# A second buffer for the first-layer products of a two-layer kernel, and two pieces of the attention's last product joined

## The chip, the cores and the metric

The kernel runs on one core of a Trainium2 chip. The metric is the device time of one execution in microseconds (us): 613.15 us is the median of three runs (611.65 to 616.95) before the change.

## The reference

The input is eight sequences of 512 tokens, 128 wide. Two layers follow each other. In both, the input is normalised and the result is `x + s * silu(g)`.

```python
xn = layernorm(x)
# first layer: 16 heads of 8, causal, with q and k through low-rank weights
s = softmax(mask(q @ k.T / sqrt(8))) @ v
h = gelu(xn @ w1 + b1)                      # 8 experts of 64
g = sum_e gates_e * (h_e @ w2_e + b2_e)     # the two best experts of each token
x = x + s * silu(g)
xn = layernorm(x)
# second layer: a delta rule over the tokens, one state per sequence
for t: y_t = W q_t;  W = W - 0.01 * (W k_t - v_t) k_t^T
s = norm(x) + y;  g = xn @ sign(weight).T
x = x + s * silu(g)
```

## The kernel before, in words

Work is staged by sequence. One iteration of the schedule works on several sequences at once: on `cur` it does the attention's exponentials and the products with the values, on `nxt`, one sequence ahead, the row maxima, the gates and the first-layer products, on `second`, two ahead, the first normalisation and the products q and k, on `prev` and `older` the second layer. Seven iterations use PLAN (cur is sequence 0 to 6); the head, FIRST_PLAN and LAST_PLAN stand around them.

An iteration has four groups of heads, and each group ten units. One unit is a block of scores of `nxt` for the maxima (`s_unit`, bank ps_s, line 930; VectorE takes its maxima, line 1457) and a block of scores of `cur` for the exponentials (`e_unit`, bank ps_e, lines 903 to 911; ScalarE's exponential, line 1251, writes prob). Both banks have two halves, so TensorE can be two units ahead of VectorE or ScalarE and no more.

The other work is cut into pieces, and PLAN says behind which unit (group, unit) each piece stands. Every engine runs its own share of the pieces in this one order; semaphores tie the engines together. A step (4, n) stands behind the last unit of group 3. SyncE issues all DMAs in the same order.

The pieces that the change and the prediction touch:

- pv0, pv1, pv2 (`pv`, line 939): probabilities times values of one group into bank ps_v, in three pieces, which need the exponentials of the units up to 3, 7 and 9. `yt` (line 955) turns the sums once two groups are in them; ahead of it ps_v is copied to yT, by ScalarE behind group 1 (line 1257), by VectorE behind group 3 (line 1470).
- h0 to h3 (`h`, lines 849 and 1227): one product of 512 columns each into ps_a, copied with a bias into the tile hid by ScalarE (line 1230). gelu (line 1232) then works on hid as a whole, at (4, 0).
- gb0 to gb3 (`gb`, lines 856 and 1438): the gates spread over the experts, multiplied into hid by VectorE. `out` (line 860) multiplies hid by the second weights. gt (line 841) is the gates turned.
- ps_a is one bank. Its users (A_PIECES: xnt, q, k, logits, gt, m_rows, h, v, gb, out) follow each other in the order of the schedule, and each waits until the one before it has been read.
- lev_a and lev_d, c_gram, c_u, c_y, c_r, c_kt and so on are the second layer. lev_d5 on VectorE (lines 1526 to 1531) is followed by low_blocks (line 1541, two copies), for which lev_a6 on TensorE (line 1041) waits. c_u's product is copied to u_sb by ScalarE (line 1313) for c_y (line 1109).
- k (line 820) is cast by ScalarE (line 1204) and its rest taken by VectorE (line 1401), then POOL. From the parts the stacks qst and kst of `second` are written and read back by DMA (`load_stacks`, line 439); the first unit of the next iteration waits for them.

Of the kernel before, what the change touches and what calls it, by code (L numbers as in the profile page):

```python
# [99 lines left out]
PLAN_CURRENT = ("gb0", "gb1", "gb2", "gb3", "out", "pv0", "pv1", "pv2", "yt", "x1", "m_rows1", "zero_state")  # L100
# [42 lines left out]
def iteration(second, nxt, cur, prev, older, plan=PLAN):  # L143

    for step in range(1 + max(at[0] for at in plan)):
        for u in range(UNITS):
            if step < GROUPS:
                yield "unit", (cur, nxt, step, u)
            for name in plan.get((step, u), []):
# [47 lines left out]
def two_layers(nc, x_in, W_dq, W_uq, W_dkv, W_uk, W_uv, W_o, w1_in, b1_in, w2_in, b2_in, cent_in, route_in,  # L197
# [8 lines left out]
    with ExitStack() as ctx:  # L206
# [511 lines left out]
        def _(pe):  # L718
# [383 lines left out]
            def c_y(b, c):  # L1102
# [11 lines left out]
                elif c == NT - 1 - (b.c == SEQS - 1):  # L1114
# [20 lines left out]
        def _(act):  # L1135
# [174 lines left out]
            def c_u(b, c):  # L1310
# [332 lines left out]
```

## Time and profile before

| | |
|---|---|
| median of three runs | 613.15 us (611.65 to 616.95) |
| the profiled execution | 617.68 us, its span 616.0 us |
| TensorE matmuls | 580.8 us busy (94%) |
| TensorE weight loads (overlap matmuls) | 389.4 us (63%) |
| VectorE | 391.8 us (64%) |
| ScalarE | 351.9 us (57%) |
| POOL | 171.7 us (28%) |
| mean granted TensorE clock | 0.982 |
| chain that ended last | TensorE 79%, VectorE 11%, ScalarE 4%, issue 2% |

Busy times are of the whole span. They are averages over groups that are limited by different things, so the stages of one iteration are read one by one below. PE is TensorE's matmuls, PEld its weight loads, DVE VectorE, ACT ScalarE. A matmul with float32 operands stands in the trace as two instructions.

### The profile page before, as it was taken

What the parts mean: (1) busy time and instruction counts of PE and PEld (TensorE: products, weight loads), DVE (VectorE), ACT (ScalarE), POOL (GpSimd) and SP (SyncE); (2) the same over time, 40 slices, a digit from 0 to 9 for tenths busy, and PEclk for the clock granted to TensorE, in tenths of its full rate; (3) what the DMA queues carried; (4) which work ended last, traced back from release to release, by engine and by line L of the source; (5) the groups of instructions that cost most, each with busy time, mean ns of one, the idle gap of its engine ahead of it and who ended that gap; (6) DMA issues with size and microseconds to landing.
All of it is one profiled execution on the core that took longest, in us unless ns stands there. A gap on an engine that the chain in (4) does not pass through costs nothing.

```text
span 616.0 us, 17485 instructions
## 1 busy us (share of the span) xinstructions
PE 580.8 (94%) x7289; PEld 389.4 (63%) x7289; DVE 391.8 (64%) x975; ACT 351.9 (57%) x679; POOL 171.7 (28%) x335
## 2 busy tenths in 40 slices
PE   7799989899998999899999999899998999799897
PEld 3345564567575766677666766678576777565565
DVE  4488765767667676867666685767666675412453
ACT  4412556755675476756675466656675476676231
POOL 7157022412224221432223230432224200311121
PEclk9999999999998999999998999799998999999899
DMA  4766293847252115410362014410361000000001
GB/s 113 162 153 132 44 84 90 157 63 63 74 116 48 43 29 114 97 43 10 87 118 60 10 45 98 95 44 5 83 128 41 10 12 1 26 18 2 3 3 35
DMA packets 58163, 39.42 MB, mean 64 GB/s; under 512 B 17957, under 2 KB 57988, under 8 KB 58084
## 3 DMA queue, kind: packets, MB, share of 16 engines
q1 hardware_dynamic: 58051, 38.29, 30.9%
q8 instruction: 58, 0.95, 0.7%
q14 instruction: 22, 0.17, 0.1%
q10 hardware_dynamic: 32, 0.01, 0.0%
HBM read 24.46 MB, written 9.96 MB: 56 GB/s over the span
## 4 chain that ended last, share of the span: by engine, by line
PE 79%; DVE 11%; ACT 4%; issue 2%; DMA 1%; POOL 1%; SPq 0%; DVEq 0%; POOLq 0%
PE ps_v L950 13%; PE ps_s L930 11%; PE ps_e L911 6%; PE ps_a L865 5%; PE ps_a L851 4%; PE ps_c L1015 4%; DVE cand L1457 4%; PE ps_e L903 3%; PE ps_e L907 3%; PE ps_e L738 3%; PE ps_a L820 3%; PE ps_s L933 2%; PE ps_c L1099 1%; PE ps_c L997 1%; PE ps_c L984 1%
## 5 line engine op out<-in xcount | busy, mean ns | idle before, releaser
L1457 DVE TENSOR_REDUCE cand<-ps_s 128x4 f32<-128x512 f32 (+1 forms) x320 | 213.4, 685 | 74.4 <-PE ps_s L933 45.4
L1251 ACT ACTIVATE prob<-ps_e 128x512 f32<-128x512 f32 x320 | 188.4, 598 | 97.2 <-PE ps_e L911 55.7
L930 PE MATMUL ps_s<-kst,qst 72*128 72x128 bf16 (+2 forms) x1024 | 126.4, 236 | 15.8 <-DVE cand L1457 12.0
L930 PEld LDWEIGHTS ps_s<-kst,qst 72*128 72x128 bf16 (+1 forms) x1024 | 72.1, 98 | 77.5 <-DVE cand L1457 36.5
L911 PE MATMUL ps_e<-qst,kst 75*128 75x256 bf16 (+3 forms) x416 | 105.3, 284 | 0.0
L950 PE MATMUL ps_v<-prob,vaug 128*32 128x512 f32 (+3 forms) x1024 | 90.6, 455 | 0.0
L903 PE MATMUL ps_e<-identb,negmask 128*128 128x150 bf16 (+3 forms) x320 | 73.2, 229 | 3.7 <-ACT prob L1251 3.3
L907 PE MATMUL ps_e<-qst,kst 128*128 128x128 bf16 x384 | 75.8, 223 | 0.0
L911 PEld LDWEIGHTS ps_e<-qst,kst 75*128 75x128 bf16 x416 | 40.9, 98 | 3.5
L738 PE MATMUL ps_e<-identb 128*128 128x512 bf16 x115 | 40.5, 408 | 1.9 <-POOL identb L520 1.9
L907 PEld LDWEIGHTS ps_e<-qst,kst 128*128 128x128 bf16 x384 | 38.4, 100 | 4.6 <-issue 0.3
L903 PEld LDWEIGHTS ps_e<-identb,negmask 128*128 128x128 bf16 x320 | 31.5, 99 | 14.6 <-ACT prob L1251 9.8
L950 PEld LDWEIGHTS ps_v<-prob,vaug 128*32 128x32 f32 x1024 | 24.1, 109 | 25.9 <-issue 20.3
L933 PE MATMUL ps_s<-negmask,identb 128*128 128x300 bf16 (+1 forms) x128 | 40.3, 315 | 0.0
L1015 PEld LDWEIGHTS ps_c<-second 32*32 32x32 f32 x2072 | 25.0, 107 | 21.3 <-issue 15.8
L649 POOL CAST mparts<-nm 128x32 bf16<-128x32 f32 x16 | 3.4, 211 | 121.8 <-DVE nm L1464 121.8
L865 PEld LDWEIGHTS ps_a<-w2s,hid 128*128 128x128 f32 x256 | 31.1, 192 | 7.1 <-issue 5.9
L1015 PE MATMUL ps_c<-second 32*32 32x32 f32 x2072 | 32.8, 194 | 2.5 <-DVE second L1520 1.6
L851 PE MATMUL ps_a<-xnT,w1s 128*128 128x512 f32 x64 | 33.5, 605 | 1.3 <-ACT hid L1230 0.8
L865 PE MATMUL ps_a<-w2s,hid 128*128 128x128 f32 x256 | 33.4, 283 | 0.7 <-ACT mrow L1243 0.7
L1230 ACT ACTIVATE hid<-ps_a,vecT 128x512 f32<-128x512 f32 x32 | 22.0, 687 | 17.1 <-PE ps_a L851 17.1
L687 POOL TENSOR_TENSOR second<-second,second_flat 128x512 f32<-128x512 f32 x7 | 8.9, 1266 | 60.2 <-ACT second_flat L1272 46.3
(340 smaller groups left out, 929.9 us busy)
## 6 DMA issues: line engine op xcount, KB each, us to landing
qst<-q_scratch SPq DMA_DIRECT2D x48, 192.0 KB
kst<-k_scratch SPq DMA_DIRECT2D x48, 192.0 KB
q_scratch<-qparts SPq DMA_DIRECT2D x24, 128.0 KB, 2.3
k_scratch<-kparts SPq DMA_DIRECT2D x24, 128.0 KB, 2.3
x_res<-in_L_attn_x_dram SPq DMA_DIRECT2D x8, 256.0 KB, 3.7
xn<-in_L_attn_x_dram SPq DMA_DIRECT2D x7, 256.0 KB, 3.5
out_dram<-second SPq DMA_DIRECT2D x7, 256.0 KB, 2.4
max_scratch<-mrow SPq DMA_DIRECT2D x16, 96.0 KB, 2.1
```

Of the source, the lines that this page charges most:

```text
L738: mm(ps_e[:, 1, :].rearrange("p (a c) -> p a c", c=P), identb[:, :], bcast(identb[:, :], 1, 4), start=True, stop=True, skip_group_check=True)
L851: mm(ps_a[:, :], w1s[:, 2 * c:2 * c + 2, :].rearrange("p e f -> p (e f)"), xnT[b.parity][:, :], start=True, stop=True)\
L865: mm(ps_a[:, tok(i)], hid[:, c, tok(i)], w2s[:, c, :], start=(i == 0 and c == 0), stop=False, skip_group_check=True)
L903: mm(diag, negmask[:, :], bcast(identb[:, masked:P], 1, len(todo)), start=True, stop=False, skip_group_check=True)
L907: last = mm(ps_e[:, bank, at:at + P], k[:, hd, tok(j)], q[:, hd, tok(j)], start=False, stop=True, skip_group_check=True)
L911: last = mm(ps_e[:, bank, at + own:at + TOK - P * j], k[0:SROWS, hd, tok(j)], q[0:SROWS, hd, P * j + own:TOK], start=False, stop=True, ski ...
L930: last = mm(ps_s[:, bank, w * n:w * (n + 1)], q[0:rows, hd, tok(i)], k[0:rows, hd, keys[0]:keys[1]], start=(n == 0), stop=True, skip_group ...
L933: last = mm(ps_s[:, bank, :].rearrange("p (a c) -> p a c", a=GH)[:, :, masked:P], identb[:, :], bcast(negmask[:, masked:P], 1, GH), start= ...
L950: last = mm(ps_v[32 * hh:32 * hh + 32, P * j:TOK], vaug[:, j, head_of(grp, hh), :], prob[:, u, o:o + TOK - P * j], start=(j == 0 and grp % ...
L1015: last = mm(bank[SQ * col:SQ * col + SQ, SQ * i:SQ * i + SQ], lhsT(row, col, i), rhs[SQ * row:SQ * row + SQ, i, :], start=True, stop=True, ...
L1251: af(prob[:, u, :], ps_e[:, u % 2, :], ACT.Exp).then_inc(S["e_emptied"], 1)
L1457: vec.tensor_reduce(cand[:, i, h0:h0 + FILLS * (len(hds) - 1) + 1:FILLS, S_SLOT[u]], ps_s[:, u % 2, :].rearrange("p (a c) -> p a c", a=len ...
```

## The change

The tile hid becomes two tiles, used in turn by sequence. With that, the four h pieces of `nxt` no longer have to wait until `out` of `cur` has read hid, and they move from group 3 to group 0. gb0 to gb3, out, xn2_norm, c_xn2t and gt move to later slots, v to one earlier. pv1 and pv2 are joined to one piece, pv12, which stands behind unit 2 of the next group (behind group 3: in (4, 1), after v). LAST_PLAN keeps pv1 and pv2 apart. The head and FIRST_PLAN stay as they are.

```diff
 PLAN = {
-    (0, 0): ["c_u3"], (0, 1): ["gb0"], (0, 2): ["ln2_stats", "c_y3"], (0, 4): ["ln2_rstd", "hn_norm"],
-    (0, 6): ["pv0"], (0, 7): ["c_ht", "rn", "c_out"], (0, 8): ["gb1"], (0, 9): ["pv1", "c_kt", "c_qt"],
-    (1, 0): ["load_x", "m_rows1"], (1, 1): ["c_vk", "gb2"], (1, 2): ["c_gram", "pv2"], (1, 3): ["logits"],
-    (1, 4): ["yt", "gb3", "xn2_norm", "gates"], (1, 5): ["lev_a1", "gate_norm"], (1, 6): ["pv0", "out"], (1, 7): ["lev_d1"], (1, 8): ["c_xn2t"],
-    (1, 9): ["pv1", "lev_a2", "gt"], (2, 0): ["ln1_stats", "lev_d2", "ln1_rstd", "m_parts0"], (2, 1): ["c_ffn"], (2, 2): ["ln1_norm", "lev_a3", "pv2"], (2, 3): ["lev_d3"],
+    (0, 0): ["c_u3"], (0, 1): ["h0"], (0, 2): ["ln2_stats", "c_y3", "h1"], (0, 3): ["h2"], (0, 4): ["ln2_rstd", "hn_norm", "h3"],
+    (0, 6): ["pv0"], (0, 7): ["c_ht", "rn", "c_out"], (0, 8): ["gb0"], (0, 9): ["c_kt", "c_qt"],
+    (1, 0): ["load_x", "m_rows1"], (1, 1): ["c_vk", "gb1"], (1, 2): ["c_gram", "pv12"], (1, 3): ["logits"],
+    (1, 4): ["yt", "gb2", "gates"], (1, 5): ["lev_a1", "gate_norm"], (1, 6): ["pv0", "gb3", "xn2_norm"], (1, 7): ["lev_d1"], (1, 8): ["out"],
+    (1, 9): ["lev_a2", "c_xn2t"], (2, 0): ["ln1_stats", "lev_d2", "ln1_rstd", "m_parts0"], (2, 1): ["c_ffn"], (2, 2): ["ln1_norm", "lev_a3", "pv12"], (2, 3): ["gt", "lev_d3"],
     (2, 4): ["yt", "m_rows0"], (2, 5): ["lev_a4", "xnt"], (2, 6): ["pv0", "q", "lev_d4"], (2, 7): ["turned0"], (2, 8): ["lev_a5", "k"],
-    (2, 9): ["pv1", "lev_d5", "turned1"], (3, 0): ["stacks0", "h0", "low_blocks"], (3, 1): ["lev_a6"], (3, 2): ["h1", "lev_d6", "pv2"], (3, 3): ["c_u0"],
-    (3, 4): ["h2", "yt", "c_y0"], (3, 5): ["c_r1"], (3, 6): ["pv0", "c_u1"], (3, 7): ["c_y1", "h3"], (3, 8): ["c_r2"],
-    (3, 9): ["c_u2", "pv1"], (4, 0): ["m_parts1", "gelu", "stacks1"], (4, 1): ["pv2", "c_y2"], (4, 2): ["v"], (4, 3): ["yt", "x1", "c_r3"],
+    (2, 9): ["lev_d5", "turned1"], (3, 0): ["stacks0", "low_blocks"], (3, 1): ["lev_a6"], (3, 2): ["lev_d6", "pv12"], (3, 3): ["c_u0"],
+    (3, 4): ["yt", "c_y0"], (3, 5): ["c_r1"], (3, 6): ["pv0", "c_u1"], (3, 7): ["c_y1"], (3, 8): ["c_r2"],
+    (3, 9): ["c_u2"], (4, 0): ["m_parts1", "gelu", "stacks1"], (4, 1): ["v", "pv12", "c_y2"], (4, 3): ["yt", "x1", "c_r3"],
 }
...
-        hid = sb("hid", [P, NC, TOK])
+        hid = [sb(f"hid{p}", [P, NC, TOK]) for p in range(2)]
...
-            def pv(b, grp, piece):
-                if piece == 0:
+            def pv(b, grp, pieces):
+                if 0 in pieces:
...
-                pe.wait_ge(S["e_emptied"], b.count(GROUPS * UNITS, UNITS * grp + (4, 8, 10)[piece]))
-                for j, u0, at in (((0, 0, 0),), ((1, 4, 0), (3, 4, 384)), ((2, 8, 0),))[piece]:
+                pe.wait_ge(S["e_emptied"], b.count(GROUPS * UNITS, UNITS * grp + (4, 8, 10)[pieces[-1]]))
+                for j, u0, at in [tile for n in pieces for tile in (((0, 0, 0),), ((1, 4, 0), (3, 4, 384)), ((2, 8, 0),))[n]]:
...
-                last.then_inc(S["pv_used"], 1)
+                last.then_inc(S["pv_used"], len(pieces))
```

In `h`, `gelu`, `gb` and `out_piece`, `hid` becomes `hid[b.parity]`.

## Rows read from the trace of the kernel before

**Rows 1.** The page, busy time, share of the span and instructions of each engine.

```profile
PE 580.8 (94%) x7289; PEld 389.4 (63%) x7289; DVE 391.8 (64%) x975; ACT 351.9 (57%) x679; POOL 171.7 (28%) x335
```

**Rows 2.** Busy time by stage: stretch, its length, busy us, PEclk, DMA share, GB/s.

```profile
114.60:127.40 12.80, 11.25 (x99) 6.52 (x97) 9.62 (x24) 8.65 (x15) 6.01 (x8) 1.00 0.63 112
251.00:264.30 13.30, 11.51 (x114) 7.22 (x112) 10.51 (x27) 8.64 (x16) 6.54 (x9) 1.00 0.36 84
299.70:318.40 18.70, 18.70 (x181) 13.27 (x180) 11.18 (x24) 12.93 (x22) 1.88 (x5) 1.00 0.49 104
318.40:333.30 14.90, 13.12 (x115) 7.62 (x113) 10.67 (x27) 8.74 (x16) 6.57 (x9) 0.89 0.41 75
387.40:403.80 16.40, 14.61 (x115) 8.90 (x113) 10.74 (x27) 9.03 (x16) 6.61 (x9) 0.79 0.33 67
```

**Rows 3.** Timeline, group 0 of cur 4: start us, duration us, instruction, [idle before <-releaser].

```profile
320.63 0.10 PEld L903 LDWEIGHTS ps_e<-identb,negmask 128*128 128x128 bf16 x1 [0.30 <-ACT prob L1251]
...
322.78 0.66 DVE L1593 TENSOR_TENSOR second<-ps_c,second 128x512 f32<-128x512 f32 x1
...
324.09 0.39 PE L930 MATMUL ps_s<-kst,qst 72*128 72x256 bf16 x2 [1.67 <-DVE cand L1457]
```

**Rows 4.** Timeline, group 3: a last piece alone, then both pieces, each with what follows.

```profile
304.26 0.64 PE L950 MATMUL ps_v<-prob,vaug 128*32 128x256 f32 x8
...
304.83 0.40 PE L930 MATMUL ps_s<-kst,qst 128*128 128x128 bf16 x4
...
314.33 1.50 PE L950 MATMUL ps_v<-prob,vaug 128*32 128x384 f32 x24
...
315.76 0.49 PE L1109 MATMUL ps_c<-u_sb,vk 128*128 128x128 f32 x2
```

**Rows 5.** Timeline from k's product (2,8) to lev_a6 (3,1), TensorE and VectorE.

```profile
296.19 1.12 PE L820 MATMUL ps_a<-xnT,w_k 128*128 128x512 f32 x2
...
297.15 0.39 PE L930 MATMUL ps_s<-kst,qst 72*128 72x128 bf16 x4
...
297.77 1.07 PE L950 MATMUL ps_v<-prob,vaug 128*32 128x384 f32 x16
...
298.06 0.69 DVE L1401 TENSOR_TENSOR krest<-ps_a,kparts 128x512 f32<-128x512 f32 x1 [0.78 <-ACT kparts L1204]
...
298.67 0.68 DVE L1457 TENSOR_REDUCE cand<-ps_s 128x4 f32<-128x512 f32 x1
298.77 0.59 PE L1015 MATMUL ps_c<-second 32*32 32x32 f32 x24
...
299.92 1.02 PE L851 MATMUL ps_a<-xnT,w1s 128*128 128x512 f32 x2
...
300.77 0.39 PE L930 MATMUL ps_s<-kst,qst 128*128 128x128 bf16 x4
...
300.94 0.45 DVE L1541 COPY second<-second 32x128 f32<-32x128 f32 x2
...
301.49 0.66 PE L1041 MATMUL ps_c<-second 64*64 64x64 f32 x8
```

**Rows 6.** Timeline, h3 and ScalarE's copy of it.

```profile
311.55 1.02 PE L851 MATMUL ps_a<-xnT,w1s 128*128 128x512 f32 x2
...
312.62 0.69 ACT L1230 ACTIVATE hid<-ps_a,vecT 128x512 f32<-128x512 f32 x1 [0.82 <-PE ps_a L851]
```

**Rows 7.** Timeline behind group 3: VectorE's copy of ps_v, and v.

```profile
315.90 0.69 DVE L1470 COPY yT<-ps_v 128x512 f32<-128x512 f32 x1 [1.06 <-PE ps_v L950]
...
316.31 1.06 PE L829 MATMUL ps_a<-w_v,xnT 128*128 128x128 f32 x8
```

**Rows 8.** Timeline, step (3,4): the copy of c_u0's product, and h2.

```profile
306.14 0.26 ACT L1313 COPY u_sb<-ps_c 128x128 f32<-128x128 f32 x1
...
306.19 1.07 PE L851 MATMUL ps_a<-xnT,w1s 128*128 128x512 f32 x2
```

**Rows 9.** Timeline, TensorE, first unit of the iteration with cur 1.

```profile
114.27 0.38 PE L930 MATMUL ps_s<-kst,qst 128*128 128x128 bf16 x4 [1.01 <-issue]
```

More of the change, by code:

```diff
@@ L99 @@
 PLAN_OLDER = ("c_u3", "c_y3", "c_out")
-PLAN_CURRENT = ("gb0", "gb1", "gb2", "gb3", "out", "pv0", "pv1", "pv2", "yt", "x1", "m_rows1", "zero_state")
+PLAN_CURRENT = ("gb0", "gb1", "gb2", "gb3", "out", "pv0", "pv1", "pv2", "pv12", "yt", "x1", "m_rows1", "zero_state")
 SEQUENCES = 8
@@ L159, in iteration @@
                 if of is not None:
-                    yield name, (of, step) if name in ("pv0", "pv1") else (of, step - 1) if name in ("pv2", "yt") else (of,)
+                    yield name, (of, step) if name in ("pv0", "pv1") else (of, step - 1) if name in ("pv2", "pv12", "yt") else (of,)
 def schedule():
@@ L864, in out_piece @@
                     for c in range(NC):
-                        mm(ps_a[:, tok(i)], hid[:, c, tok(i)], w2s[:, c, :], start=(i == 0 and c == 0), stop=False,
+                        mm(ps_a[:, tok(i)], hid[b.parity][:, c, tok(i)], w2s[:, c, :], start=(i == 0 and c == 0), stop=False,
                            skip_group_check=True)
@@ L1117, in _ @@
             pieces = {"xnt": xnt, "q": lambda b: qk(b, 0), "k": lambda b: qk(b, 1), "v": v, "logits": logits, "gt": gt,
-                      "out": out_piece, "m_rows0": lambda b: m_rows(b, 0), "m_rows1": lambda b: m_rows(b, 1), "pv0": lambda b, grp: pv(b, grp, 0), "pv1": lambda b, grp: pv(b, grp, 1), "pv2": lambda b, grp: pv(b, grp, 2), "yt": yt, "c_xn2t": c_xn2t, "c_ht": c_ht, "c_kt": c_kt,
+                      "out": out_piece, "m_rows0": lambda b: m_rows(b, 0), "m_rows1": lambda b: m_rows(b, 1), "pv0": lambda b, grp: pv(b, grp, (0,)), "pv1": lambda b, grp: pv(b, grp, (1,)), "pv2": lambda b, grp: pv(b, grp, (2,)), "pv12": lambda b, grp: pv(b, grp, (1, 2)), "yt": yt, "c_xn2t": c_xn2t, "c_ht": c_ht, "c_kt": c_kt,
                       "c_qt": c_qt, "c_vk": c_vk, "c_gram": c_gram, "c_ffn": c_ffn}
@@ L1229, in h @@
                 after(act, S["gelu_ready"], b.count(1, 0))
-                af(hid[:, c, :], ps_a[:, :], ACT.Identity, bias=vecT[:, c:c + 1]).then_inc(S["a_emptied"], 1)
+                af(hid[b.parity][:, c, :], ps_a[:, :], ACT.Identity, bias=vecT[:, c:c + 1]).then_inc(S["a_emptied"], 1)
             def gelu(b):
                 act.wait_ge(S["a_emptied"], A_NUMBER[b.c, "h3"] + 1)
-                af(hid[:, :, :], hid[:, :, :], ACT.Gelu).then_inc(S["gelu_ready"], 1)
+                af(hid[b.parity][:, :, :], hid[b.parity][:, :, :], ACT.Gelu).then_inc(S["gelu_ready"], 1)
             def out_piece(b):
@@ L1315, in _ @@
             pieces = {"xnt": xnt, "q": lambda b: split_hi(b, 0), "k": lambda b: split_hi(b, 1), "v": v, "gates": gates, "gt": gt,
-                      "gelu": gelu, "out": out_piece, "m_rows0": lambda b: m_rows(b, 0), "m_rows1": lambda b: m_rows(b, 1), "pv2": pv, "c_xn2t": c_xn2t, "c_ht": c_ht, "c_kt": c_kt,
+                      "gelu": gelu, "out": out_piece, "m_rows0": lambda b: m_rows(b, 0), "m_rows1": lambda b: m_rows(b, 1), "pv2": pv, "pv12": pv, "c_xn2t": c_xn2t, "c_ht": c_ht, "c_kt": c_kt,
                       "c_qt": c_qt, "c_gram": c_gram, "c_ffn": c_ffn}
@@ L1440, in gb @@
                 dve.wait_ge(S["gelu_ready"], b.count(1, 1))
-                vec.tensor_tensor(hid[:, c, :], hid[:, c, :], ps_a[:, :], ALU.mult).then_inc(S["a_emptied"], 1)
+                vec.tensor_tensor(hid[b.parity][:, c, :], hid[b.parity][:, c, :], ps_a[:, :], ALU.mult).then_inc(S["a_emptied"], 1)
             def out_piece(b):
```

2 lines of the change are left out of this document (1 added, 1 removed).

## The prediction

> **What bounds the kernel now.** I read the busy shares first: TensorE is busy for 94% of the span, so time is won only where it stands idle, where its clock is low, or where its work shrinks [rows 1]. Then the stages of one iteration of the plan (busy time by stage): group 3 is full to the last tenth (18.70 of 18.70 us), group 0 is not (11.51 of 13.30). The granted clock is 1.00 in all of them but four group 0 stretches: 0.89 in three, 0.79 in one [rows 2]. A stretch at 0.89 takes 14.90 us against 13.30, the one at 0.79 takes 16.40: together 3 x 1.6 + 3.1 = 7.9 us lost to the clock.
>
> The timeline of group 0 shows the hole. Behind the third unit VectorE does the statistics of the residual, then c_y3's addition (0.66 us), and only then the maxima for which the sixth unit waits: TensorE stands idle for 1.67 us. The same gap is there in five iterations (cur 2 to 6), and in four of them the clock then fell. A smaller gap, 0.30 us, stands ahead of unit 2's mask product: ScalarE is late after gelu and its table loads [rows 3].
>
> **The change, term by term.** Matmuls are moved, not saved: four h products, one gt, one gb leave one group for another. Only waits, the clock and the joins count.
>
> *Joins.* A middle piece alone takes 1.00 us from its start to the next product (297.77 to 298.77), a last piece 0.57 (304.26 to 304.83), both in a row 1.43 (314.33 to 315.76) [rows 4, 5]. Group 3 has them in a row already. So 3 groups x 7 iterations save 0.14 each: **-2.9 us** (bounds 0 and, by busy time, 1.07 + 0.64 - 1.50 = 0.21 each, -4.4).
>
> *Group 0 gets the h's.* They fill both gaps: -1.97 us. But hid has two buffers and ps_a still one bank. From an h product's start to its copy by ScalarE is 1.07 us, the copy 0.69, a release about 0.05: h can follow h after 1.8 us [rows 6], while the work between, one h (0.85) and one unit (0.6), is 1.45 [rows 5]. So h2 and h3 wait 0.35 each, h1, with c_y3 ahead of it, 0.15: +0.85. And v now stands ahead of pv12. Before, v covered VectorE's copy of yT (0.69, begun 0.14 after c_y2's start) ahead of the transposes yt; now only c_y2's two products do (0.55): +0.35 [rows 4, 7]. Net -0.8, times 5; cur 1 has other gaps, I take -0.4: **-4.4** (bounds -8, if nothing new waits, and 0).
>
> *Group 3 loses the h's, and pv1 goes from (2,9) to (3,2).* This decides. lev_a6 in (3,1) needs low_blocks, VectorE's two copies, and already starts 0.10 us after them (301.39 to 301.49), in every iteration with a k behind it (cur 1 to 5). Back from there is a chain which the change doesn't touch: k's product 296.19, ScalarE's cast, VectorE's rest (298.06), the maxima of unit (2,9) (298.67), lev_d5's three, the maxima of (3,0), the copies. It takes 5.30 us. TensorE's work in that stretch was just that long; without pv1 (1.00) and h0 (0.85) it is 0.96 + 0.62 + 1.15 + 0.72 = 3.45 [rows 5]. So 1.85 us is not saved but waited, about 0.5 ahead of unit (3,1)'s first product (it needs the maxima of (2,9)), the rest ahead of lev_a6: 5 x 1.85 = 9.2. cur 6 has no k: between 0 and 1.85, I take 1.0, since the rest and the cast drop out. h1 and h3 come out at full value. Behind h2 stands c_y0, which needs the copy of u that ends 306.40, while TensorE would be there at 306.19: +0.25, times 6, 1.5 [rows 8]. Together **+11.7** (bounds 2, if VectorE ran ahead, and 14).
>
> *The first iteration (cur 0).* Its group 3 ends in a wait of 1.01 us for a release that the view does not name; the code's wait there is for the stacks of sequence 2 [rows 9]. Their start hangs on k, not on group 3. What leaves group 3 (four h 3.4, pv1 1.0, less the join's 0.9 and the yt wait) is then waited: +3.2, and the three waits among h's in group 0 add 0.8: **+4.0** (bounds 0, if gaps in groups 1 and 2 take it up, and 5).
>
> *At nothing.* gb, xn2_norm, out, c_xn2t one or two slots later: VectorE catches up under out's products; without that cover, at most 0.35 an iteration, 2 us in all. gt in (2,3) has m_rows0 a unit behind. On SP the load of x_res goes with gb0 past the store of c_out and its wait for POOL: load_x and the row maxima's write then stand behind one more issue, and all three are used a group or more later. POOL's order is unchanged. ScalarE's wait for pieces at unit 4 stands behind the joined piece in TensorE's order, so it adds none.
>
> The Trainium skill (TensorE: Matmul & The Clock Gate, section "A second HAM failure mode: psum-queue depth-cycling") says that brief idles between groups of matmuls, come by in cycling through PSUM banks, can be frequent enough to make the clock swing. By that rule the h's, turning about one bank, would keep group 0's low clock; by the rows, where short gaps left it at 1.00, they would not.
>
> **Rivals.**
> 1. *The clock holds in group 3*: the split stalls are too short. +8.4 - 7.9 + 1.6 = +2.1, 615.3 to 619.8: 617. For it: no contiguous gap there reaches 1.67. Against: some 1.85 us idle within 2.6. Chance 0.24.
> 2. *The stall at lev_a6 does not come, and it is faster.* VectorE would have to reach low_blocks some 1.8 us sooner, which it can only if k's cast and rest come sooner against TensorE. Its place is 298.06 to 301.39. Then the third term is 1.5, or some 2: -2.9 - 4.4 + 2 + 4.0 - 7.9 + 1.6 = -7.6, 605.6 to 610: 607. It decides from a stall under 0.5. Against: five of five iterations show copies and lev_a6 0.10 to 0.15 apart. That h's in group 3 took ScalarE from that chain is not so: h0's copy comes after it. Chance 0.16.
> 3. *The clock falls after every lev_a6 stall*: 2.5 x 1.6 more: 625. Chance 0.15.
> 4. *The clock falls in group 0 all the same*, by a run of short gaps between h's: six times 1.6 on the forecast, 631. (This is what the page's rule would do.) Against: gap by gap there is 0.4 or less. Chance 0.05.
> That the change doesn't do what it says: in group 3 the join joins nothing, and it is counted so.
>
> **The numbers.** Forecast 621, chance 0.40; by itself 617 to 626. About 1% (607.0 to 619.3) is what a measurement here can't tell from no change. Within it lie rival 1 (0.24), the low end of the forecast (0.05) and what of rival 2 ends above 607 (0.06): 0.35. Slower: 0.35 + 0.15 + 0.05 = 0.55. Faster: 0.10. The range 611 to 629 leaves out most of rival 2 and rival 4.
>
> **What would show it.** In the profile after: lev_a6 still 0.1 us behind low_blocks, with idle TensorE before it, some 1.8 us in group 3 of cur 1 to 5; group 0 with h products 1.8 us apart, no 1.67 us gap, clock 1.00; the third and second piece 24 in a row in all groups, 1.43 us; a wait of about 4 us ahead of cur 1's first unit; yt waiting about 0.35 us for yT. Wrong, if group 3 has TensorE busy throughout, or if the clock in it stays at 1.00 after each stall.

## The result, and the profile after

The changed kernel is slower, by 1.5 to 1.8%. In the first set its four runs gave 632.89 us in the median (622.68 to 637.33) beside 615.05 for the kernel before (611.65 to 617.18); two of the four, the profiled one among them, lie more than 1.5% above the fastest and are left out of the ratio, 1.0178 (95% interval 1.0115 to 1.0241). A second set gave 622.66 (621.30 to 628.74) beside 615.06, ratio 1.0147 (1.0092 to 1.0201). The forecast was 621 with a range of 611 to 629: the side and the second set are in it, and so is the mean of the first set's two other runs, 625.9; the first set's median is not. So there are two things to explain: why it is slower at all, and why the same kernel takes 622 us in one execution and 637 in another.

The profiled execution took 636.67 us (span 634.9, before 616.0). The page of the changed kernel, first the engines' busy time (it answers to [rows 1]), then the granted clock in 40 slices:

```profile
PE 591.2 (93%) x7289; PEld 399.4 (63%) x7289; DVE 394.4 (62%) x975; ACT 350.1 (55%) x679; POOL 170.7 (27%) x335
...
PEclk9899999899979998999979998999979999999999
```

The stages of the changed kernel (stretch, length, busy us of the engines, PEclk, DMA share, GB/s), in order: group 0 of cur 1, group 0 and group 3 of cur 3, group 0 and group 3 of cur 4. They answer to [rows 2]:

```profile
118.40:133.90 15.50, 15.13 (x91) 8.32 (x89) 9.40 (x23) 9.81 (x17) 4.83 (x7) 0.89 0.55 93
267.30:281.80 14.50, 14.02 (x107) 8.33 (x105) 10.33 (x26) 10.83 (x19) 6.50 (x9) 1.00 0.32 55
316.80:338.40 21.60, 19.79 (x189) 14.17 (x188) 12.13 (x27) 11.21 (x21) 2.67 (x6) 0.84 0.48 103
338.40:352.90 14.50, 14.02 (x107) 8.31 (x104) 10.34 (x26) 10.83 (x19) 6.50 (x9) 1.00 0.25 53
387.90:408.20 20.30, 18.30 (x190) 13.13 (x188) 12.12 (x27) 11.19 (x21) 2.67 (x6) 0.92 0.49 110
```

The picture of [rows 2] is turned round. Group 0, four h pieces longer, now runs at 1.00 in cur 2 to 6. Group 3, which was full before (18.70 of 18.70), has 1.8 to 2.0 us without TensorE and runs at 0.84 or 0.92 in all five iterations cur 1 to 5. Its length in cur 3 is 21.6 us although four h pieces have left it.

The timeline of the changed kernel (start, duration, instruction, idle before it and what ended it) shows, in order: the wait that opens cur 1, a hole in the middle of lev_a2's products in cur 1, three of the h pieces in group 0 of cur 3, then the chain from k to lev_a6 and the transposes yt at the end of that group 3.

```profile
115.16 0.66 PE L960 MATMUL ps_v<-ident,yT 128*128 128x128 f32 x4 [0.81 <-DVE yT L1470]
118.09 0.38 PE L930 MATMUL ps_s<-kst,qst 128*128 128x128 bf16 x4 [2.28 <-issue]
...
151.89 0.45 PE L1015 MATMUL ps_c<-second 32*32 32x32 f32 x30
155.31 0.24 PE L1015 MATMUL ps_c<-second 32*32 32x32 f32 x2 [2.97 <-issue]
...
268.72 1.02 PE L851 MATMUL ps_a<-xnT,w1s 128*128 128x512 f32 x2
...
270.52 1.13 PE L851 MATMUL ps_a<-xnT,w1s 128*128 128x512 f32 x2
...
272.42 1.13 PE L851 MATMUL ps_a<-xnT,w1s 128*128 128x512 f32 x2 [0.17 <-ACT hid L1230]
...
314.29 1.12 PE L820 MATMUL ps_a<-xnT,w_k 128*128 128x512 f32 x2
...
316.17 0.69 DVE L1401 TENSOR_TENSOR krest<-ps_a,kparts 128x512 f32<-128x512 f32 x1 [0.78 <-ACT kparts L1204]
...
316.78 0.68 DVE L1457 TENSOR_REDUCE cand<-ps_s 128x4 f32<-128x512 f32 x1
...
316.40 0.40 PE L930 MATMUL ps_s<-kst,qst 128*128 128x128 bf16 x4
...
317.52 0.40 PE L930 MATMUL ps_s<-kst,qst 128*128 128x128 bf16 x4 [0.34 <-DVE cand L1457]
...
319.04 0.45 DVE L1541 COPY second<-second 32x128 f32<-32x128 f32 x2
...
319.60 0.65 PE L1041 MATMUL ps_c<-second 64*64 64x64 f32 x8 [1.30 <-issue]
320.18 0.58 PE L930 MATMUL ps_s<-kst,qst 128*128 128x128 bf16 x4
...
322.48 2.79 PE L950 MATMUL ps_v<-prob,vaug 128*32 128x384 f32 x24
...
336.25 0.49 PE L1109 MATMUL ps_c<-u_sb,vk 128*128 128x128 f32 x2
...
337.13 0.66 PE L960 MATMUL ps_v<-ident,yT 128*128 128x128 f32 x4 [0.17 <-DVE yT L1470]
```

From k's product to lev_a6 it is 319.60 - 314.29 = 5.31 us, against 5.30 in [rows 5]: the chain on VectorE is what it was, and TensorE, with pv1 and h0 gone from between, waits for it twice, with 0.34 and 1.30 us of idle time. These figures count from the end of the product before, which the profile models; counted from start to start, less the work between as [rows 5] has it (0.62 for a unit, 0.72 for the one ahead of lev_a6), the waits are 317.52 - 316.40 - 0.62 = 0.50 and 319.60 - 317.52 - 0.72 = 1.36 us. Right behind the second wait the products run at half speed: four score products take 0.58 us where [rows 4] has 0.40, and the joined pieces 2.79 where it has 1.50.

### The profile page after: what moved, and what is told of

It is laid out like the page before. It is cut to its first block, busy times and chain, and to the rows that moved or that the text cites. A ratio compares the mean times of both kernels' runs of the same rounds, so it can differ in the third digit from the quotient of the medians.

```text
span 634.9 us, 17485 instructions
## 1 busy us (share of the span) xinstructions
PE 591.2 (93%) x7289; PEld 399.4 (63%) x7289; DVE 394.4 (62%) x975; ACT 350.1 (55%) x679; POOL 170.7 (27%) x335
## 4 chain that ended last, share of the span: by engine, by line
PE 77%; DVE 7%; ACT 7%; issue 4%; DMA 2%; POOL 1%; SPq 0%; ACTq 0%; DVEq 0%
PE ps_v L950 13%; PE ps_s L930 11%; PE ps_e L911 6%; PE ps_a L865 5%; PE ps_a L851 5%; PE ps_c L1015 3%; PE ps_s L933 3%; PE ps_e L903 3%; PE ps_e L907 3%; PE ps_e L738 2%; ACT hid L1230 2%; ACT prob L1251 2%; PE ps_a L820 2%; PE ps_c L997 1%; PE ps_c L1099 1%
## 5 line engine op out<-in xcount | busy, mean ns | idle before, releaser
L930 PEld LDWEIGHTS ps_s<-kst,qst 72*128 72x128 bf16 (+1 forms) x1024 | 75.3, 100 | 74.9 <-DVE cand L1457 31.2
L950 PE MATMUL ps_v<-prob,vaug 128*32 128x512 f32 (+3 forms) x1024 | 89.0, 468 | 0.0
L907 PE MATMUL ps_e<-qst,kst 128*128 128x128 bf16 x384 | 74.3, 220 | 0.0
L950 PEld LDWEIGHTS ps_v<-prob,vaug 128*32 128x32 f32 x1024 | 26.9, 115 | 24.9 <-issue 21.1
L933 PE MATMUL ps_s<-negmask,identb 128*128 128x300 bf16 (+1 forms) x128 | 42.5, 332 | 0.0
L851 PE MATMUL ps_a<-xnT,w1s 128*128 128x512 f32 x64 | 36.2, 647 | 4.2 <-ACT hid L1230 3.5
L1230 ACT ACTIVATE hid<-ps_a,vecT 128x512 f32<-128x512 f32 x32 | 22.0, 687 | 22.0 <-PE ps_a L851 21.7
```

The source lines that it names most:

```text
L851: mm(ps_a[:, :], w1s[:, 2 * c:2 * c + 2, :].rearrange("p e f -> p (e f)"), xnT[b.parity][:, :], start=True, stop=True)\
L907: last = mm(ps_e[:, bank, at:at + P], k[:, hd, tok(j)], q[:, hd, tok(j)], start=False, stop=True, skip_group_check=True)
L930: last = mm(ps_s[:, bank, w * n:w * (n + 1)], q[0:rows, hd, tok(i)], k[0:rows, hd, keys[0]:keys[1]], start=(n == 0), stop=True, skip_group ...
L933: last = mm(ps_s[:, bank, :].rearrange("p (a c) -> p a c", a=GH)[:, :, masked:P], identb[:, :], bcast(negmask[:, masked:P], 1, GH), start= ...
L950: last = mm(ps_v[32 * hh:32 * hh + 32, P * j:TOK], vaug[:, j, head_of(grp, hh), :], prob[:, u, o:o + TOK - P * j], start=(j == 0 and grp % ...
```

## The experiments

Entries of the plan that stay as they are, are left out of the diffs.

**Undoing one half of the change each.** The theory: the stall ahead of lev_a6 is the sum of the two pieces taken from between, h0 and pv1. The first kernel is the changed one with the four h pieces back in group 3.

```diff
-    (0, 1): ["h0"], (0, 2): ["ln2_stats", "c_y3", "h1"], (0, 3): ["h2"], (0, 4): ["ln2_rstd", "hn_norm", "h3"],
+    (0, 2): ["ln2_stats", "c_y3"], (0, 4): ["ln2_rstd", "hn_norm"],
...
-    (3, 0): ["stacks0", "low_blocks"], (3, 2): ["lev_d6", "pv12"], (3, 4): ["yt", "c_y0"], (3, 7): ["c_y1"],
+    (3, 0): ["stacks0", "h0", "low_blocks"], (3, 2): ["h1", "lev_d6", "pv12"], (3, 4): ["h2", "yt", "c_y0"], (3, 7): ["c_y1", "h3"],
```

> The changed plan with the four h pieces back in their old slots of group 3, the joined piece and all else as changed. Theory A (the loss is idle time ahead of lev_a6, which VectorE's chain from k sets, and the low clock behind it): h0's 0.85 us covers that stall again, pv1's 1.0 does not; so 0.9 to 1.0 us idle ahead of lev_a6 in cur 1 to 5, the 1.67 us hole of group 0 back, no wait of over 1.1 us at the start of cur 1. About 3 us slower than before to 3 us faster (joins -2.9, stall +5, less low clock in group 3 than in the changed kernel). Theory B (the loss is the h's turning about one bank in group 0): as before or faster by the joins, 612 or less, and the stall ahead of lev_a6 plays no part.

Measured: 621.61 us (614.78 to 626.92), ratio 1.0076 (1.0031 to 1.012). The second kernel keeps the h pieces in group 0 and takes the join apart again.

```diff
-    (0, 9): ["c_kt", "c_qt"], (1, 2): ["c_gram", "pv12"], (1, 9): ["lev_a2", "c_xn2t"], (2, 2): ["ln1_norm", "lev_a3", "pv12"],
-    (2, 9): ["lev_d5", "turned1"], (3, 2): ["lev_d6", "pv12"], (3, 9): ["c_u2"], (4, 1): ["v", "pv12", "c_y2"],
+    (0, 9): ["pv1", "c_kt", "c_qt"], (1, 2): ["c_gram", "pv2"], (1, 9): ["pv1", "lev_a2", "c_xn2t"], (2, 2): ["ln1_norm", "lev_a3", "pv2"],
+    (2, 9): ["pv1", "lev_d5", "turned1"], (3, 2): ["lev_d6", "pv2"], (3, 9): ["c_u2", "pv1"], (4, 1): ["v", "pv2", "c_y2"],
```

> The changed plan with pv1 and pv2 apart again in their old slots, the h pieces in group 0 as changed. Theory A: pv1 in (2,9) covers 1.0 us of the 1.85, so about 0.85 us idle is left ahead of lev_a6, too short for the clock to fall there; group 0 stays filled at a clock of 1.00; the wait at the start of cur 1 stays over 2 us. About 612 to 617, well below the changed kernel. Theory B (the bank in group 0): no better than the changed kernel's fast runs, 622 and more. Theory C (joining as such costs, by a longer stretch of TensorE without a unit): faster than the changed kernel, with the stall ahead of lev_a6 as long as there.

Measured: 620.38 us (618.26 to 620.78), ratio 1.0048 (1.001 to 1.0087). The timeline of the kernel with the h pieces back, the sixth unit of group 0, then the unit ahead of lev_a6 and lev_a6 of the same iteration:

```profile
256.44 0.39 PE L930 MATMUL ps_s<-kst,qst 72*128 72x256 bf16 x2 [1.88 <-DVE cand L1457]
...
299.12 0.39 PE L930 MATMUL ps_s<-kst,qst 128*128 128x128 bf16 x4
...
300.83 0.65 PE L1041 MATMUL ps_c<-second 64*64 64x64 f32 x8 [0.95 <-issue]
```

And of the kernel with the pieces apart, two h pieces in group 0, then the unit ahead of lev_a6 and lev_a6:

```profile
264.25 1.13 PE L851 MATMUL ps_a<-xnT,w1s 128*128 128x512 f32 x2 [0.17 <-ACT hid L1230]
...
266.16 1.12 PE L851 MATMUL ps_a<-xnT,w1s 128*128 128x512 f32 x2 [0.26 <-ACT hid L1230]
...
310.25 0.39 PE L930 MATMUL ps_s<-kst,qst 128*128 128x128 bf16 x4
...
311.83 0.65 PE L1041 MATMUL ps_c<-second 64*64 64x64 f32 x8 [0.81 <-issue]
```

Counted from start to start as above, lev_a6 waits 0.99 us without pv1 (idle 0.95), 0.86 without h0 (idle 0.81), and 0.50 + 1.36 = 1.86 without both: the parts add up, and the prediction had 1.00 + 0.85. That shows where the stall comes from. In neither kernel did the clock fall in group 3. Each half of the change is slower by itself, in the median by less than the whole. Both times are misses: I expected 612 to 618 and 612 to 617. In the profile of the second kernel an undisturbed iteration takes 68.1 us against 67.4 to 67.5 before, and cur 0 and cur 1 are 4.4 and 2.9 us longer than before; the largest differences lie in those two. The second time lies between what theories A and B gave and does not decide between them; the rows do, with the stall as theory A had it.

**Taking the stall away from VectorE's side.** The changed kernel with the two copies low_blocks issued ahead of k's rest.

```diff
-    (2, 7): ["turned0"], (3, 0): ["stacks0", "low_blocks"],
+    (2, 7): ["low_blocks", "turned0"], (3, 0): ["stacks0"],
```

> The changed kernel with VectorE's two copies low_blocks moved from (3,0) to (2,7), where VectorE is idle; they need lev_d4 alone. Nothing else is touched, and TensorE's order is the same. Theory A: lev_a6 then waits only for lev_d5's first operation, so the gap ahead of it goes from 1.27 us to 0.2 or less in cur 1 to 5, the clock holds in group 3, and the kernel is at 606 to 612, faster than both. Theory B (the bank in group 0) and theory C (the join): 622 or more, since neither is touched.

Measured: 622.14 us (616.88 to 624.34), ratio 1.0111 (1.0076 to 1.0146): a miss. Its timeline in group 3 of one iteration:

```profile
306.61 0.40 PE L930 MATMUL ps_s<-kst,qst 128*128 128x128 bf16 x4 [0.23 <-DVE cand L1457]
...
307.93 0.40 PE L930 MATMUL ps_s<-kst,qst 128*128 128x128 bf16 x4 [0.54 <-DVE cand L1457]
...
308.64 0.68 PE L1041 MATMUL ps_c<-second 64*64 64x64 f32 x8
...
309.60 0.40 PE L930 MATMUL ps_s<-kst,qst 128*128 128x128 bf16 x4 [0.28 <-DVE cand L1457]
```

lev_a6 no longer waits, but the maxima behind k's rest are still as late, and the units wait for them: 0.23 + 0.54 + 0.28 us. low_blocks was the last link, not the cause: wherever the wait stands, TensorE has too little work beside VectorE's chain there. The clock stays at 1.00 in group 3 in this profile, and an iteration with cur 2 to 5 takes 67.8 us.

**Holding the clock in the stall.** The changed kernel with seven bfloat16 products of 512 columns into ps_a behind unit (3,0), read by nobody.

```diff
-    (3, 0): ["stacks0", "low_blocks"],
+    (3, 0): ["stacks0", "spare", "low_blocks"],
...
+            def spare(b):
+                pe.wait_ge(S["a_emptied"], A_NUMBER[b.c, "k"] + 1)
+                for _ in range(7):
+                    mm(ps_a[:, :].rearrange("p (a c) -> p a c", c=P), identb[:, :], bcast(identb[:, :], 1, 4), start=True, stop=True,
+                       skip_group_check=True)
```

> The changed kernel with seven products of 512 columns (bfloat16, into the free bank ps_a, read by nobody) behind unit (3,0) for cur 0 to 5. No wait goes and no work is saved; they only keep TensorE busy in the stall ahead of lev_a6. Theory A with the clock: the stall's idle time shrinks to 0.3 or less, the clock stays at 1.00 in group 3, lev_a6 starts as late after k as in the changed kernel: 615 to 619, below the changed kernel although it does more. If the low clock in group 3 has another cause, it stays, and the time is that of the changed kernel, 623 to 637.

Measured: 624.63 us (623.96 to 626.66), ratio 1.0145 (1.0104 to 1.0185). Two stretches of it, group 3 of cur 3 and the whole iteration with cur 3:

```profile
314.30:333.10 18.80, 18.14 (x197) 13.18 (x196) 12.18 (x27) 11.24 (x21) 2.67 (x6) 1.00 0.53 118
...
264.80:333.10 68.30, 67.08 (x916) 48.30 (x914) 48.40 (x121) 42.78 (x83) 19.21 (x34) 1.00 0.28 64
```

The clock stays at 1.00 in group 3 of cur 2 to 5, and the four runs spread over 2.7 us where those of the changed kernel spread over 14.7 and 7.4 in its two sets. That fits a spread that goes with the clock in group 3, but does not show it: the kernel with low_blocks early held that clock in its profile too, and its six runs spread over 7.5. And the median is above the 615 to 619 that I expected, and no lower than that of the second set of the changed kernel: a miss. With the clock held, an iteration takes 68.3 us against 67.4 before. This kernel, too, had a hole in lev_a2 of cur 1, 3.45 us long, with the lower clock behind it: its cur 0 and cur 1 take 59.3 and 76.5 us, against 55.5 and 67.4 in the profile of the kernel before. These 12.9 us are more than the 8.9 by which its whole span is longer. So the clock in group 3 is not all that makes the change slow.

**The changed kernel again**, unaltered.

> The changed kernel once more, unaltered, to see how often its clock falls behind the stall at lev_a6. My theory: the stall of 1.25 us and the smaller one of 0.3 us ahead of it are there in cur 2 to 5 of every execution; what differs between executions is for how long the clock is at 0.5 behind them, so the time goes down as the mean granted clock goes up, 622 us at 0.995 and 636 us at 0.967. Rival (the time differs for another reason, such as the wait that opens cur 1): an execution whose profile has a clock above 0.985 still takes over 630 us.

Measured: 622.66 us; the profiled execution 622.25, span 620.5. Group 3 of cur 2, 3 and 4 in it, then the whole iteration with cur 5:

```profile
237.00:258.70 21.70, 19.89 (x190) 14.10 (x189) 12.18 (x27) 11.25 (x21) 2.68 (x6) 0.84 0.48 102
308.10:328.50 20.40, 18.40 (x191) 13.21 (x189) 12.24 (x27) 11.30 (x21) 2.68 (x6) 0.92 0.52 110
377.90:396.70 18.80, 16.80 (x191) 12.41 (x188) 12.18 (x27) 11.24 (x21) 2.68 (x6) 1.00 0.53 118
396.70:465.00 68.30, 65.74 (x909) 47.54 (x907) 48.43 (x121) 42.79 (x83) 19.26 (x34) 1.00 0.27 64
```

In all three stretches of group 3 TensorE idles 1.8 to 2.0 us (in cur 4, with the clock at 1.00, it is 0.34 and 1.30 ahead of lev_a6, as in cur 3 of the first profile), and yet the clock fell for long, for short and not at all: 21.7, 20.4 and 18.8 us. That gives the price of a fall from rows, 1.6 or 2.9 us. The hole in lev_a2 is not there in this execution. My expectation that time goes by the clock alone holds only in part: 621.30 us stands beside a clock of 0.994 and 622.25 beside 0.982.

**The clock's share in the kernel before.** The kernel before with the same seven products (they wait for gb0 here) in the hole of group 0.

```diff
-    (0, 4): ["ln2_rstd", "hn_norm"],
+    (0, 4): ["spare", "ln2_rstd", "hn_norm"],
```

> The kernel before, with seven bfloat16 products of 512 columns into ps_a behind unit (0,4), read by nobody, where TensorE stood idle for 1.67 us. It has no change of the plan. My theory (the change's only large gain in group 0 was the clock): the gap is at most 0.4 us, the clock is 1.00 in group 0 of cur 2 to 6, group 0 takes 13.3 us in every iteration, the time is 606 to 610 us (five stretches of 1.6 us less at most). Rival: the clock falls elsewhere instead, or the fall cost nothing that lasts: 612 to 616 us.

Measured: 612.06 us (610.21 to 612.35), ratio 0.9941 (0.9921 to 0.9961), above the 606 to 610 that I expected and in the range of the rival. Group 0 of cur 1 and of cur 5, and the iteration with cur 3:

```profile
116.30:130.30 14.00, 12.60 (x106) 7.18 (x104) 10.40 (x26) 9.71 (x17) 6.39 (x8) 1.00 0.49 110
...
387.40:400.80 13.40, 13.13 (x122) 7.92 (x120) 10.59 (x27) 8.75 (x17) 6.57 (x9) 1.00 0.38 80
...
252.50:320.00 67.50, 67.10 (x917) 47.74 (x914) 47.87 (x121) 43.03 (x83) 19.35 (x34) 1.00 0.28 64
```

An iteration is as long as an undisturbed one before, the clock is at 1.00 in all of cur 1 to 6, and group 0 of cur 2 to 6 takes 13.4 us, where the profiled execution before had 14.8, 13.4, 14.9, 16.4 and 14.9: its four falls cost 7.5 us, close to the 7.9 that the prediction read there. The time fell by less for two reasons that are not the clock's in these groups. The products also stand in cur 1, where the gaps are smaller, and group 0 of cur 1 takes 14.0 us against 12.8 in [rows 2]. And cur 0 began 1.5 us later in this execution than in the other, so that the profiled span is only 5.6 us shorter. In the median, filling the hole was worth 3.0 us net of its cost in cur 1, some 4.3 without it (an estimate from the two rows).

**Moving only as much as the hole holds.** The changed kernel with two h pieces in group 0 and two in group 3, and with pv1 and pv2 of group 2 apart in their old places.

```diff
-    (0, 1): ["h0"], (0, 2): ["ln2_stats", "c_y3", "h1"], (0, 3): ["h2"], (0, 4): ["ln2_rstd", "hn_norm", "h3"],
+    (0, 2): ["ln2_stats", "c_y3", "h0"], (0, 3): ["h1"], (0, 4): ["ln2_rstd", "hn_norm"],
...
-    (2, 9): ["lev_d5", "turned1"], (3, 0): ["stacks0", "low_blocks"], (3, 2): ["lev_d6", "pv12"], (3, 4): ["yt", "c_y0"], (4, 1): ["v", "pv12", "c_y2"],
+    (2, 9): ["pv1", "lev_d5", "turned1"], (3, 0): ["stacks0", "h2", "low_blocks"], (3, 2): ["lev_d6", "pv2"], (3, 4): ["h3", "yt", "c_y0"], (4, 1): ["pv12", "c_y2"], (4, 2): ["v"],
```

> The changed kernel, but only two of the four h pieces go to group 0 (h0 behind unit (0,2) and h1 behind (0,3), where the gap ahead of the sixth unit was); h2 stands in group 3 where h0 was (3,0), h3 where h2 was (3,4). pv1 of group 2 is back at (2,9) and pv2 at (3,2); the other two groups keep the joined piece. My theory (the changed kernel is slow because TensorE has nothing to do while VectorE goes from k's rest to low_blocks, and because its clock falls in that gap): lev_a6 waits 0.1 us or less in cur 1 to 5, the gap of 1.67 us in group 0 is filled, the clock stays at 1.00 in both groups, an iteration without a fallen clock takes 65.5 to 66.5 us against 67.4 before, the time is 600 to 608 us. Rival A (the gain is eaten by the turn about the bank ps_a and by VectorE's later start in group 1): the stall at lev_a6 goes and the clock holds, but an iteration takes 67 us or more, the time is 610 to 614 us. Rival B (the stall of some 3 us inside lev_a2 of cur 1 and the wait that opens cur 1 are what costs): the time stays above 616 us.

Measured: 606.05 us (602.62 to 606.49), ratio 0.9845 (0.9811 to 0.988): 1.5% faster than the kernel before, and faster than the changed one. The copies and lev_a6 in its timeline, and the iteration with cur 3:

```profile
302.32 1.02 PE L851 MATMUL ps_a<-xnT,w1s 128*128 128x512 f32 x2
...
303.35 0.45 DVE L1541 COPY second<-second 32x128 f32<-32x128 f32 x2
...
303.90 0.66 PE L1041 MATMUL ps_c<-second 64*64 64x64 f32 x8
```

```profile
253.90:319.60 65.70, 64.98 (x908) 47.32 (x906) 48.20 (x121) 42.73 (x83) 19.35 (x34) 1.00 0.29 67
```

lev_a6 follows the copies by 0.1 us after their end and waits for nothing; the iteration is 1.7 us shorter than an undisturbed one before, and TensorE is idle for 0.7 us of it. The iterations cur 2 to 6 all stand at 1.00. Three things differ from the changed kernel at once (two h pieces, pv1 of group 2, the place of v), so the run does not say what each is worth; both rivals fell with it.

The same kernel with group 2's pieces joined at (3,2) and low_blocks at (2,7):

```diff
-    (2, 7): ["turned0"], (2, 9): ["pv1", "lev_d5", "turned1"], (3, 0): ["stacks0", "h2", "low_blocks"], (3, 2): ["lev_d6", "pv2"],
+    (2, 7): ["low_blocks", "turned0"], (2, 9): ["lev_d5", "turned1"], (3, 0): ["stacks0", "h2"], (3, 2): ["lev_d6", "pv12"],
```

> As the kernel with two h pieces in group 0, but group 2's middle and last piece are joined at (3,2) as in the changed kernel, and VectorE's two copies low_blocks go from behind (3,0) to behind (2,7), ahead of k's rest in VectorE's order. My theory: lev_a6 no longer hangs on the chain from k, so the joined piece costs no stall, and the join gives 0.14 us an iteration: 599 to 608 us, the same as the kernel with two h pieces or 1 us below it. Rival A: TensorE then waits for the maxima of unit (2,9) ahead of unit (3,1), which hang on the same rest of k: a gap of 0.5 us there and 0.3 us in group 2, and 3 to 5 us more than the kernel with two h pieces.

Measured: 604.47 us (602.25 to 605.39), ratio 0.9826 (0.9796 to 0.9857), not to be told from the one above. Its iteration takes 66.1 us, 0.4 more and not 0.14 less: of the rival's waits the one in group 2 came (0.3 us there). What its profiled execution gains, 2.7 us, lies ahead of cur 0, which began 3.9 us earlier, and in cur 1 (0.7 us), not in the join.

**The hole in lev_a2 of cur 1.** The trace puts no releaser to it ("issue"). In the stretch around it (148 to 156 us of the first profile) the DMA queues of the changed kernel hold:

```profile
q1 hardware_dynamic: 2487, 0.63, 92.3%
q8 instruction: 1, 0.02, 1.3%
```

Up to the hole the DMA engines are full with the load of the constant rows of the second pair of stacks (qst from identb, kst from negmask, 1.7 MB), in the hole they are busy for 0.49 of the time, and one packet of instructions, 16 KB, is among the others. Four kernels move that load to an earlier place:

```diff
-                if half and b.c < 2:
-                    load_pads(b.parity)
+                if b.c == 0:
+                    load_pads(1 - half)
```

> The changed kernel; only the load of the constant rows of the second pair of stacks (qst from identb, kst from negmask, 1.7 MB) is issued one iteration and a half sooner, behind m_rows0 of the first sequence, so that it no longer falls into group 1 of cur 1. My theory (the stall of some 3 us inside lev_a2 of cur 1 comes because TensorE's next instructions are fetched by the same DMA engines that this load keeps full): no gap over 0.5 us in groups 1 and 2 of cur 1, and those two groups take 35.5 us, as in the execution of the changed kernel that had no such gap, against 40.1 in the one that had; the rest, with the stall at lev_a6, stays; 619 to 626 us, by the clock. Rival (the gap has to do with the order of the work in cur 1, not with this load): a gap of 1.5 to 3.5 us stays in lev_a2 or lev_a3 of cur 1, and the time is that of the changed kernel.

> The kernel with two h pieces in group 0, with the same earlier load of the constant rows. My theory: the gap of 2.66 us in group 1 of cur 1 and the low clock behind it go, 4 us in all; the iterations with cur 2 to 5 stay at 65.7 us: 600 to 604 us. Rival (the load only moves the trouble): the first iteration gets longer by as much, since the load then falls beside the loads of the head, and the time stays at 605 to 607 us.

> The kernel with two h pieces in group 0 and the copies low_blocks ahead of k's rest, with the same earlier load. Its iterations take 66.1 us against 65.7 of the kernel with the copies in their old place, its gap in cur 1 was 1.64 us. My theory: 600 to 604 us, and with equal starts 1.5 to 2 us slower than the kernel with the copies in their old place. Rival (the old place of the copies costs something at the end of the first iteration, where it was 1.5 us slower): it stays 1 to 2 us faster.

> A control: the kernel before, with the earlier load alone. Its trace had no gap in cur 1 behind that load. My theory: cur 1 stays as it was, no change within 0.4%: 613 to 616 us. Rival (the load also slows what comes after it in the kernel before, such as the wait of 0.9 us in group 0 of cur 1 or the one ahead of cur 1): 609 to 612 us.

Measured, each above what I expected: the changed kernel with it 629.15 us (626.46 to 630.83), ratio 1.0207 (1.0165 to 1.025); the one with two h pieces 604.11 (598.38 to 605.53), 0.9787 (0.9737 to 0.9837); with the early copies 605.27 (601.72 to 609.64), 0.9827 (0.9775 to 0.9878); the kernel before 619.43 (612.88 to 624.91), 1.0052 (1.0016 to 1.0087). Group 1 of cur 1 in the first of them:

```profile
130.90:150.20 19.30, 19.30 (x272) 15.37 (x270) 13.73 (x36) 9.55 (x22) 3.42 (x8) 1.00 0.03 7
```

TensorE is busy throughout, and no hole is there in any of the three profiles with h pieces in group 0; without the move it was there in five of seven (1.64 to 3.45 us; with two h pieces it stands in c_xn2t, right behind lev_a2). The hole was absent twice without the move, and no record says that TensorE waited for that packet. But the traces hold more. These are the rows from the start of the span to just ahead of the hole's end, for the changed kernel and for the one with the seven products in group 3:

```profile
0.00:155.20 155.20, 137.44 (x1104) 80.24 (x1104) 97.55 (x229) 73.32 (x135) 52.23 (x130) 0.98 0.62 105
...
0.00:157.40 157.40, 139.45 (x1104) 80.69 (x1104) 97.63 (x229) 73.31 (x135) 52.10 (x130) 0.98 0.61 104
```

In both, and with low_blocks early, TensorE has run 1104 matmuls and 1104 weight loads when it stops, in the two kernels with two h pieces 1103 and 1104, although different work stands there: the 31st of lev_a2's 32 matmuls, the 24th where seven were put in ahead, the second of c_xn2t where two h pieces fewer stand ahead. So the hole has its place in the count of TensorE's instructions, not in the order of the work, which was the rival. And in each of the five a packet of instructions lands 1.2 to 1.4 us before the hole ends; it starts 17.6 to 20.8 us after the packet before it on its queue, against 11.7 to 16.1 us in the nine profiles without a hole. That the next instructions came late is thus well supported. That the load made them late agrees with the three profiles that moved it, but why they were in time twice without the move stays open. The changed kernel did not get faster: its clock fell behind all five stalls this time (groups 1 and 2 of cur 1 take 35.4 us, as expected). And the trouble moved, as the rival had it. With two h pieces the wait that opens cur 1 is now

```profile
118.17 0.59 PE L930 MATMUL ps_s<-kst,qst 128*128 128x128 bf16 x4 [5.58 <-issue]
```

against some 1 us without the move. The intervals of the four kernels with two h pieces overlap, so none of them is shown to be the best. Why the kernel before got 0.5% slower is open.

## Why the prediction was right, and where it was wrong

**The side and the main step held.** Left aside the clock, an iteration of cur 2 to 5 was to get -0.42 (joins) - 0.8 (group 0) + 1.85 + 0.25 (group 3) = +0.88 us longer. It is 68.3 us against 67.4 in two undisturbed iterations, +0.8 from the starts to two places (68.26 and 67.47):

```profile
251.00:318.40 67.40, 65.48 (x908) 47.03 (x906) 47.76 (x121) 42.93 (x83) 19.36 (x34) 1.00 0.28 65
```

is that row of the kernel before, beside the last row of the changed kernel's second profile above. Lengths of groups and iterations are from the start of a first unit to that of the next. By groups 0 to 3 the two iterations differ by +1.07, -0.38, +0.06 and +0.04 us: group 3 is as long as before without its four h pieces. Step by step, with the waits counted from start to start as the prediction counted them:

- *Joins*, 0.14 us each: groups 1 and 2 take 0.13 less in the changed kernel than with the pieces apart (19.08 against 19.21, 15.93 against 16.06).
- *Group 0*: h follows h after 1.80 and 1.90 us (1.8 predicted). The second h, with c_y3 ahead of it, waits for nothing where 0.15 stood; the third and fourth come 0.45 us later than the 1.45 of work between them, where 0.35 stood. The transposes yt start 337.13 - 336.25 = 0.88 us behind c_y2, whose products take 0.55: they wait 0.33 us for yT, 0.35 predicted. The gap of 1.67 us is gone and the clock is 1.00 in cur 2 to 6, so rival 4 fell. The Trainium skill (TensorE: Matmul & The Clock Gate, section "A second HAM failure mode: psum-queue depth-cycling") describes brief idles, from cycling through PSUM banks, that are frequent enough to make the clock swing. Applied to the h's turn about the one bank ps_a, it would have had the clock come down; these rows, with 0.48 us idle in 14.5 us and a clock of 1.00, speak against it here.
- *Group 3*: 1.86 us of stall against 1.85 (rival 2 fell), split 0.50 and 1.36 where 0.5 and 1.35 stood; c_y0 waits 0.36 against 0.25. In cur 6, which has no k, TensorE idles 0.66 us ahead of lev_a6 and 0.54 ahead of lev_d5's products, 1.2 together where 1.0 stood.
- *The first iteration*: the waits at its end are 0.81 + 2.28 us against some 4; from the start of cur 0 to that of cur 1 it takes 57.8 us (57.6 in the second profile) against 55.5. +2.3 measured, +3.6 with the join predicted. Behind that wait the clock fell for 3.4 us, as the +1.6 of the sum had it.

**The term that was mis-sized is the clock in group 3.** The step "I take half of five, 2.5 x 1.6 = +4.0" failed in both factors. The clock fell behind 13 of the 15 stalls of three profiles (five, three, five), and it often stayed low for twice as long: with the prices from above, 1.6 + 4 x 2.9 = 13 us in the first profile and about 6 in the second (1.6 + 2.9 + 1.6). Rival 3 had all five, but at 1.6 each. The argument "no contiguous gap there reaches 1.67" was no protection: 1.30 with 0.34 a little ahead was enough. Rival 1, which rested on it, fell.

**One term was missing**: the hole of 2.97 us in cur 1 and the low clock behind it, some 5 us together in the first profile and none in the second. Nor had the sum that the head differs from one execution to the next: up to cur 0 the plan is the same in the ten kernels without the earlier load, and it takes 58.7 to 62.9 us, from 60.6 in the five profiles with the clock at 0.5 for 3.4 us near 27 us and at most 59.1 in the others. Iteration by iteration the two profiles differ from that of the kernel before as follows. First: start +1.5, cur 0 +2.3, cur 1 +10.2, cur 2 to 6 +2.4, +3.7, +0.8, +0.7, -1.3, the rest -1.2: +19.1 against 634.9 - 616.0 = +18.9. Second: -0.4, +2.0, +3.9, +2.3, +2.4, -0.8, -2.2, -1.3, -1.2: +4.7 against +4.5. In these profiles most of the loss lies in the first two iterations: in the six profiles with four h pieces in group 0, cur 0 and cur 1 together are 5.3 to 12.9 us longer than before, with none or two of them there (and the load in its place) 1.2 to 2.3.

**The gain was sized too large for the median.** The clock given back in group 0 was counted at 7.9 us, from an execution with four falls, for which it was nearly right (7.5); filling the hole alone was worth 3.0 in the median, some 4.3 without the cost in cur 1. The prediction named this (fewer low stretches leave less to win, 623.8) and took the middle. That the second set lies so near 621 is in part luck: this gain and cur 0's wait were both counted too large, with opposite signs, and the clock in group 3, counted too small, stands against an end that was 1.2 us shorter than in the profiled execution before, which had one more fall of the clock there.

## What to carry to other kernels

Work that stands between two links of another engine's chain is cover, even where TensorE is the bound: before it is moved, lay the chain's length (5.30 us) beside the work left (3.45), and move only what the other stage's hole holds. Two h pieces for a hole of 1.67 us, with pv1 of group 2 left in its place, gave -1.5%; four gave +0.5% with all pieces apart and +1.5 to +1.8% with them joined.
|---|---|---|
| 0.73 to 0.95 us | lev_a6, pieces apart and h pieces back | 0 of 10 |
| 1.00 to 1.29 us | the wait that opens cur 1, in three profiles | 0 of 3 |
| 0.28 + 1.28 to 0.34 + 1.30 us | lev_a6, changed kernel (two profiles) and with the earlier load | 13 of 15 |
| 1.67 to 1.89 us | group 0, kernel before, with the earlier load, h pieces back | 4, 2 and 2 of 5 |
| 1.36 to 5.58 us | the wait that opens cur 1, in nine profiles | 9 of 9 |
| 1.64 to 3.45 us | the hole in cur 1, in five profiles | 5 of 5 |

The same gap, at the same place of the same kernel, cost 0, 1.6 or 2.9 us. The kernels whose gaps were filled spread over 2.1 and 2.7 us (hole filled, stall filled), those with gaps over 5.9 and, in its two sets, 14.7 and 7.4. What decides between two executions stays open.
